# Routed experts taken in the rank order of their counts, with 512 to 336 slots by rank, in a kernel of power attention and a mixture of experts

## What is computed

```python
scores = softmax(x @ gate_w.T)                    # x: N = 4096 rows of D = 256; E = 64 experts
topk_w, topk_idx = top_k(scores, 6)               # 6 experts per row, weights normalized to sum 1
flat_e = topk_idx.reshape(-1)
order = argsort(flat_e); se = flat_e[order]; st = order // 6
counts = bincount(flat_e, length=E)
pos = arange(A) - offsets[se]; valid = pos < 768  # a row past slot 768 of its expert is dropped
buf[se, pos] += x[st]                             # E x 768 x 256
g, u = buf @ w_gate.T, buf @ w_up.T               # F = 176 hidden columns per expert
eo = (silu(g) * u) @ w_down.T
y[st] += eo[se, pos] * weight                     # scattered back, added
return y + shared(x)                              # one shared expert of 352 hidden columns, all rows
```

## Time and profile before

| | us |
|---|---|
| median of 3 runs | 2335.61 |
| lowest, highest | 2334.75, 2338.43 |
| span of the profiled execution | 2331.3 |
| PE busy | 2202.9 (94%) |
| PE weight loads busy | 1988.1 (85%) |
| DVE busy | 1327.8 (57%) |
| ACT busy | 1202.7 (52%) |
| POOL busy | 817.4 (35%) |

### The profile page before, as it was taken

One profiled execution on the slowest core, in us unless ns is written; L12 is line 12 of the kernel. 1 busy time (PEld: TensorE's weight loads), 2 busy tenths in 40 slices (PEclk: granted clock), 3 DMA queues, 4 the chain that ended last, 5 costly groups with the idle time before them and its releaser, 6 DMA issues.

```text
span 2331.3 us, 38666 instructions
## 1 busy us (share of the span) xinstructions
PE 2202.9 (94%) x14776; PEld 1988.1 (85%) x14776; DVE 1327.8 (57%) x2873; ACT 1202.7 (52%) x2232; POOL 817.4 (35%) x792
## 2 busy tenths in 40 slices
PE   8999999999999999999999999998888999999980
PEld 7999998998989899898988889997777888888870
DVE  3444444454655454555545475447657888888863
ACT  4545444454444454444445444444345777777763
POOL 3111112000014500002440014400445888878785
PEclk9999999999999999999999999999999999999995
DMA  5866721122113222111322213211548988898857
GB/s 179 330 256 261 298 80 60 45 61 84 50 54 119 89 57 76 54 51 59 120 85 79 66 54 100 90 61 61 185 149 267 213 203 213 195 214 194 212 70 235
DMA packets 153136, 310.61 MB, mean 133 GB/s; under 512 B 26576, under 2 KB 88272, under 8 KB 152944
## 3 DMA queue, kind: packets, MB, share of 16 engines
q1 hardware_dynamic: 104320, 251.98, 32.3%
q0 software_dynamic: 48192, 55.68, 12.3%
q10 hardware_dynamic: 432, 0.40, 0.0%
HBM read 168.01 MB, written 149.34 MB: 136 GB/s over the span
## 4 chain that ended last, share of the span: by engine, by line
PE 87%; DVE 5%; issue 3%; ACT 2%; POOL 1%; DMA 1%; another core or an unknown queue 0%; ACTq 0%; POOLq 0%; SPq 0%; DVEq 0%
PE bank L856 53%; PE bank L1219 20%; PE bank L866 8%; PE bank L1322 2%; PE bank L1232 2%; DVE ub L1724 1%; POOL y_part L2125 1%; DVE stats L2038 0%; ACT q_hi L1447 0%; POOL slots L2115 0%; ACT x1t_hi L1489 0%; POOL xt_lo L2077 0%; DMA gw_raw<-in_gw 0%; DMA y_part<-y_e,row_token 0%; DVE bank L1908 0%
## 5 line engine op out<-in xcount | busy, mean ns | idle before, releaser
L1219 PEld LDWEIGHTS bank<-v,a 128*128 128x128 f32 x4608 | 603.4, 191 | 43.8 <-ACT a L1471 0.8
L1219 PE MATMUL bank<-v,a 128*128 128x129 f32 x4608 | 616.9, 275 | 0.6 <-ACT a L1471 0.6
L2125 POOL DMA_INDIRECT y_part<-y_e,row_token x264 | 414.1, 1569 | 105.9 <-issue 85.9
L2095 POOL TENSOR_TENSOR decay_all<-decay_all,tab 128x128 f32<-128x128 f32 x128 | 60.9, 476 | 917.2 <-DMA decay_all<-decay_dram 916.8
L1467 ACT ACTIVATE a<-bank,c_s 128x512 f32<-128x512 f32 x384 | 263.0, 685 | 178.3 <-PE bank L856 163.1
L1471 ACT ACTIVATE a<-ub 128x512 f32<-128x512 f32 (+1 forms) x256 | 133.8, 524 | 377.1 <-DVE ub L1724 359.2
L2115 POOL DMA_INDIRECT slots<-rows,slot_u x192 | 188.7, 983 | 308.2 <-PE bank L1219 137.3
L856 PE MATMUL bank<-q_hi,k_hi 128*128 128x512 f32 (+1 forms) x640 | 261.8, 409 | 8.3 <-DVE ub L1724 7.3
L1703 DVE TENSOR_TENSOR q_lo<-bank,q_hi 128x512 fp32r<-128x512 f32 x128 | 88.5, 691 | 273.7 <-ACT q_hi L1447 270.3
L856 PE MATMUL bank<-q_lo,k_hi 128*128 128x512 f32 (+1 forms) x640 | 237.5, 371 | 0.0
L856 PE MATMUL bank<-q_hi,k_lo 128*128 128x512 f32 (+1 forms) x640 | 236.5, 370 | 0.0
(11 more groups left out here) (215 smaller groups left out, 4917.5 us busy)
## 6 DMA issues: line engine op xcount, KB each, us to landing
slots<-acc SPq DMA_DIRECT2D x65, 816.0 KB, 7.9
w_raw_f<-in_wffn SPq DMA_DIRECT2D x66, 624.0 KB
xr<-slots SPq DMA_DIRECT2D x64, 544.0 KB
decay_all<-decay_dram SPq DMA_DIRECT2D x128, 128.0 KB
w_hi<-w_dram SPq DMA_DIRECT2D x24, 384.0 KB
w_lo<-w_dram SPq DMA_DIRECT2D x24, 384.0 KB
sum<-y_part SPq DMA_DIRECT2D x14, 512.0 KB, 10.2
wc_hi<-wc_dram SPq DMA_DIRECT2D x24, 256.0 KB
```

Source lines behind the costliest of these rows:

```text
L1219: ins = e.matmul(dst[:, tt, r, :], a32[u % NA][:, r, t0:t0 + P], v[n % 3][:, s, :], start=(s == 0 and r == 0), stop=(s == 2 * g + tt), ski ...
L2095: e.tensor_tensor(arg[:, GROUP:GROUP + P], arg[:, P:GROUP], mask, ALU.add)
L2125: e.indirect_dma_start(out=y_part[part], out_offset=bass.IndirectOffsetOnAxis(ap=token, axis=0), in_=y_e[y][:, j, :], in_offset=None, boun ...
```

## The change

**Ranks.** When `taken` has the counts of the first seven eighths of the rows, DVE makes a key per expert (`rank_keys`: expert number minus 64 times its count). It takes the diagonal to have each expert's key on its partition, and counts the smaller keys in its row. That is the expert's rank, 0 for the fullest. A one-hot matrix of ranks goes to PE, which multiplies it with the expert numbers (`rank_experts`), and DVE copies the product out. `rank_i` then holds the expert of each rank, on one partition, for address registers, and `rank_x` the same on all partitions.

**Tiles by rank.** `TIERS` gives each rank its tiles: ranks 0 to 17 four of 128 slots, 18 to 37 four of 112, 38 to 51 three of 128, 52 to 63 three of 112. That is 512, 448, 384 and 336 slots. Ranks 0 to 3 get one more step each, of one tile of 128 (slots 512 to 639), with the weights of the step before it. `SEQ` takes wide and narrow ranks in turn: 0, its extra, 63, 1, its extra, 62, and so on, then 4, 59, 5, 58, to 31, 32: 68 steps.

**Transfers.** SP loads the rank's expert number into a register (`value_load`) ahead of each transfer of rows or weights and forms the address from it (`rows_at`, `weights_at`). The extras' rows come by such plain transfers too (`extra_in`), and all four are issued in step 0. `over_in`, its 12 fetches on POOL, `counted`'s scan and `jobs` are gone.

**General path.** In step 2, `rank_counts` multiplies the final counts out by rank on PE, and DVE compares them with the reach of each rank (640, 512, 448, 384, 336). `rest_i` says for each group of four ranks whether one of them is over, `over_count` how many are. If it is not zero, every group with an expert over its reach runs four bodies, each over the slots from its reach to 768, behind the last step. `KEPT`, the number of steps whose slot weights are kept, goes from 8 plus 4 to 12. `slots` and its filling shrink from 65 to 64 regions.

Its core:

```diff
+TIERS = [(18, 4, P), (20, 4, 112), (14, 3, P), (12, 3, 112)]
+MAIN_TILES = [(nt, pt) for n_, nt, pt in TIERS for _ in range(n_)]
+EXTRA = 4
+REACH = [nt * pt + P * (x_ < EXTRA) for x_, (nt, pt) in enumerate(MAIN_TILES)]
-OVER_AT = 18, 34, 50, E + 3
-SEQ = list(range(E))
-for i_, place_ in enumerate(OVER_AT):
-    SEQ.insert(place_, E + i_)
+MAINS = [x_ for i_ in range(E // 2) for x_ in (i_, E - 1 - i_)]
+SEQ = [y_ for x_ in MAINS for y_ in ((x_, E + x_) if x_ < EXTRA else (x_,))]
...
     route_some(3)
+    do("rank_keys")
     do("gate_up", 2, 0)
+    on_spare("rank_experts")
     route_some(2)
...
-    do("jobs", 0)
...
-        after = SEQ[place + 1:place + 4]
-        if 3 <= place < 2 + JOBS // JC:
-            do("jobs", place - 2)
-        if x_id + 2 < E:
-            do("rows_in", x_id + 2)
+        later = MAINS[NTH[x_id] + 2:NTH[x_id] + 4] if x_id < E else []
+        if later:
+            do("rows_in", later[0])
         if place == 0:
-            for i in range(KJ):
-                do("over_in", E + i)
+            for i in range(EXTRA):
+                do("extra_in", E + i)
+        if place == 2:
+            on_spare("rank_counts")
             do("load_count")
...
+            def expert_at(x_id):
+                once.wait_ge(c_rank, 1)
+                return e.value_load(rank_i[0:1, x_id % E:x_id % E + 1], min_val=0, max_val=E - 1)
+
             def rows_in(x_id):
-                e.dma_start(xr[r][:, :, :], slots[x_id * CAP:x_id * CAP + MAIN, :].rearrange(
-                    "(p j) c -> p j c", p=P)).then_inc(c_r[r], 16)
+                e.dma_start(xr[i][0:pt, 0:nt, :], rows_at(expert_at(x_id), 0, nt, pt)).then_inc(c_r[i], 16)
...
+            def down_rows(ps, k, w, tiles, pt):
+                for jj, j in enumerate(tiles):
+                    ins = down_passes(e, [(k % HS, w)], slice(j * pt, (j + 1) * pt), ps[0:pt, jj * C:(jj + 1) * C], jj == 0)
...
+            def rank_keys():
+                once.wait_ge(*out_of(("route", B - 1, "taken")))
+                step(e.scalar_tensor_tensor(out=rank_key, in0=taken[:, :], scalar=-float(E), in1=tab[:, K_IOTA:K_IOTA + E],
+                                            op0=ALU.mult, op1=ALU.add))
+                step(diagonal_sum(rank_key, rank_col[:, 0:1]))
+                steps_done()
+                step(e.tensor_scalar(rank_cmp, rank_key, rank_col[:, 0:1], None, ALU.is_lt))
+                steps_done()
+                step(e.tensor_reduce(rank_col[:, 1:2], rank_cmp, AX.X, ALU.add))
+                steps_done()
+                e.tensor_scalar(rank_hot[:, :], tab[:, K_IOTA:K_IOTA + E], rank_col[:, 1:2], None, ALU.is_equal).then_inc(c_hot)
+
+            def rank_experts():
+                once.wait_ge(s_spare, m + 1)
+                e.tensor_copy(rank_i[:, :], bank[6 + m % 2][0:1, 0:E]).then_inc(c_rank)
+                e.tensor_copy(rank_x[:, :], bank[6 + m % 2][:, 0:E]).then_inc(s_out_of[m % 2])
...
+                pt = shape_of(x_id)[1]
+                for j in tiles_in_pair(x_id, pair):
+                    add_rows(row_token[kept_at(x_id)][0:pt, j:j + 1], y_e[PLACE[x_id] % YS][0:pt, j, :], pt, part, c_add[part])
...
-            with e.If(count > KJ):
+            with e.If(count > 0):
+                for q0 in range(0, E, REST):
+                    with e.If(e.value_load(rest_i[0:1, q0 // REST:q0 // REST + 1], min_val=0, max_val=1) > 0):
+                        for q in range(q0, q0 + REST):
+                            body(q)
```

More of the change, by code:

```diff
@@ L530, in schedule @@
         do("hidden", k, 3)
-        if len(after) > 1:
-            do("split_lo", after[1], 2)
+        if later:
+            do("split_lo", later[0], 2)
         if place:
@@ L536, in schedule, with shape_of, pairs_of, tiles_in_pair @@
     return order, spare
+def shape_of(x_id):
+    return MAIN_TILES[x_id] if x_id < E else (1, P)
 def tiles_of(x_id):
-    return MT if x_id < E else OVER_TILES
+    return shape_of(x_id)[0]
+def pairs_of(x_id):
+    return (tiles_of(x_id) + 1) // 2
+def tiles_in_pair(x_id, pair):
+    return range(2 * pair, min(2 * pair + 2, tiles_of(x_id)))
 def before_job(x_id, count):
@@ L607, in build @@
     N_SPLIT = len(split_at)
-    down_of = {x_id: spare["down", x_id, tiles_of(x_id) // 2 - 1] for x_id in range(E + KJ)}
+    down_of = {x_id: spare["down", x_id, pairs_of(x_id) - 1] for x_id in SEQ}
     shared_down_of = {m: spare["shared_down", m, 1] for m in range(M)}
@@ new lines, in over_body @@
+                for i, tiles in enumerate(pairs):
+                    e.wait_ge(s_spare, m + i + 1)
+                    turned_hi(bank[6 + (m + i) % 2], 0, tiles, pt)
+                e.wait_ge(o_rest[q // REST], rest_moved(q) + 32)
+                e.activation(wf_hi[w][:, :], w_rest_raw[:, :], ACT.Copy).then_inc(c_wh)
+                for part in range(4):
+                    hidden_part(k, part, nt * pt)
+                e.wait_ge(c_pick, STEPS + q + 1)
+                md = m + len(pairs)
@@ L1594, in over_skip_banks, with over_skip @@
-            def over_skip_banks(first, count):
-                for q in range(first, first + count):
-                    for j in range(OVER_TILES):
-                        e.sem_inc(s_out_of[(over_m(q) + 1 + j) % 2], 1)
+            def over_skip(first, last):
+                e.sem_inc(c_xh, (over_m(last) - over_m(first)) // 2)
+                e.sem_inc(c_wh, last - first)
+                e.sem_inc(c_silu, 2 * (last - first))
+                e.sem_inc(c_hh, 2 * (last - first))
+                for i in range(2):
+                    e.sem_inc(s_out_of[i], rest_downs(first, last, i))
@@ L1951, in pick_weights @@
-            def pick_weights(nth_, x_rows, n, expert, out_):
-                once.wait_ge(c_pick, nth_)
-                step(e.scalar_tensor_tensor(out=of_expert[:, 0:n, :], in0=x_rows[:, 0:n, ID_COL:ID_COL + TOPK], scalar=expert,
-                                            in1=x_rows[:, 0:n, W_COL:W_COL + TOPK], op0=ALU.is_equal, op1=ALU.mult))
-                steps_done()
-                e.tensor_reduce(out_[:, 0:n], of_expert[:, 0:n, :], AX.X, ALU.add).then_inc(c_pick)
+                diagonal_sum(taken[:, :], count_col[:, :]).then_inc(c_hot)
@@ new lines, in rank_counts @@
+            def rank_counts():
+                m = spare["rank_counts",]
+                once.wait_ge(s_spare, m + 1)
+                e.tensor_tensor(rank_over[:, :], bank[6 + m % 2][0:1, 0:E], tab[0:1, K_REACH:K_REACH + E], ALU.is_gt).then_inc(
+                    s_out_of[m % 2])
+                once.wait_ge(*out_of(("rank_counts",)))
+                e.tensor_reduce(rest_i[:, :], rank_over[:, :].rearrange("p (g r) -> p g r", r=REST), AX.X, ALU.max)
+                step(e.tensor_reduce(rank_col[0:1, 0:1], rank_over[:, :], AX.X, ALU.add))
+                steps_done()
+                e.tensor_copy(over_count[:, :], rank_col[0:1, 0:1]).then_inc(c_count)
@@ L2010, in over_body @@
+                e.wait_ge(o_step, q + 1)
+                e.tensor_reduce(row_w[KEPT][0:pt, 0:nt], of_expert[0:pt, 0:nt, :], AX.X, ALU.add).then_inc(c_pick)
+                for part in range(4):
+                    hidden_part(k, part, nt * pt)
+                for i in range(len(pairs)):
+                    e.wait_ge(s_out_of[(m + i) % 2], (m + i) // 2 + 1)
+                e.wait_ge(c_wl, N_SPLIT + q + 1)
+                e.wait_ge(c_pick, STEPS + q + 1)
                 e.wait_ge(c_h, 2 * (k + 1))
@@ L2219, in pool_program @@
             all_sent(once)
-        FILLS = [(slots[ex * CAP:(ex + 1) * CAP, :], slot0[:, :, :]) for ex in range(E + 1)]
+        FILLS = [(slots[ex * CAP:(ex + 1) * CAP, :], slot0[:, :, :]) for ex in range(E)]
         N_FILL = len(FILLS)
@@ L2345, in constants @@
     t[:, K_IOTA:K_IOTA + E] = np.arange(E)
-    for i, first in enumerate((MAIN, MAIN + P, 0)):
-        t[:, K_ROW + i] = first + np.arange(P)
+    t[:, K_REACH:K_REACH + E] = [reach if reach < CAP else N for reach in REACH]
+    t[0:E, K_EXPERT] = np.arange(E)
     return t
```

479 lines of the change are left out of this document (233 added, 246 removed).

## The result

The change takes 2281.7 us (median of 4 runs, 2278.4 to 2282.8) where the kernel before takes 2336.2: a ratio of 0.9767, 95% interval 0.9752 to 0.9781. So 54 us went, where I forecast 75. The measured time lies inside the range (2244 to 2286), next to its upper end, and 10 us from the first rival's 2272 against 22 from the forecast.

The account below looks back on a forecast made before the run. PE was taken to bound the kernel, four others within 20%. PE -68.5, POOL's tail -12.9 and the ranks +6 sum to -75.4 us, from 2335.6 to 2260 us; range 2244 to 2286.

Parts of the forecast that it names:

- the first rival: Routed experts: POOL's add costs the same at 112 rows as at 128; 2272 us, chance 0.25.
- PE's part, -68.5: Routed experts: fewer columns and no `jobs` cut PE's work to 431 us, 68.5 us less.
- The prices on the line: PE's products of 448, 384 and 336 columns start 0.204, 0.176 and 0.154 us apart, between the 256- and 512-column prices.
- 0.111 for 128 columns: PE's products in the extra steps: 0.111 us each, from a 129-column product in attention; the line would give 0.063.
- TensorE at 1.2 GHz inside the expert part: Sign listed under what would show the forecast wrong: PE at the lower clock during the routed experts.
- The ranks, +6: Ahead of the routed experts: DVE waits for PE's rank product, so the layer norm's statistics start 6.6 us later; +6 us.
- POOL's tail, -12.9: From PE's last gate-and-up product to the flag behind the last add: shrinks from 33.4 to 20.5 us.
- 2.6 us of leftover lag: End of the routed part: POOL's remaining lag, counted as 2.6 us within the 20.5 us tail.
- The fixed add: POOL in the routed part: an add of 112 rows costs as much as one of 128; 2272 us, chance 0.25.
- DVE's round: Three-tile steps: DVE's round stays at 6.58 us however few the slots; 2290 us, chance 0.1.
- The general path: Behind the last step: one expert over its rank's reach costs four bodies, 88 us; 2348 us, chance 0.03.
- DMA work: DMA engines in the routed part: work falls with rows and adds to about 370 us of 431.

Follow-up runs that it names:

- d1: The kernel before, unchanged, measured and traced again on the chip of the third batch: 0.9986 of the kernel before's time.
- d2: The change, unchanged, measured and traced again on the chip of the third batch: 0.9780 of the kernel before's time.
- a2: The change with its pairs of ranks reversed, from the middle outwards (31, 32 first, 0 and 63 last): 0.9731 of the kernel before's time.
- a4: The change with one add of rows left out for each of the 20 experts with four tiles of 112: 0.9687 of the kernel before's time.
- b1: The change with ranks in their own order, 0 to 63, instead of wide and narrow in turn: 0.9812 of the kernel before's time.
- a1: The change with PE's product for the ranks ahead of gate_up(2, 0) instead of behind it: 0.9761 of the kernel before's time.
- a3: The change with tiles of 128 where it has 112, the same 234 adds: 0.9785 of the kernel before's time.
- d3: The change with four tiles of 128 (512 slots) for every rank, on the third batch's chip: 0.9998 of the kernel before's time.

## Why the prediction was right, and where a step failed

- **PE's part, -68.5: measured -64.5.** The prices on the line held (0.20, 0.18, 0.16 us), and so did 0.111 for 128 columns. A pair of 448-column steps is cheaper than I had it (13.58 for 13.86), one of 512 and 336 dearer (12.85 for 12.66). What was missing are waits in the first steps: 4.21 us for the first extra's rows, for which I had 3, 1.66 for `xe_lo` behind the extra, and 3.4 for evictions, for which I had 1. The sign "TensorE at 1.2 GHz inside the expert part" was seen, from 1769.4 to 1779.6, where the granted clock is 0.50. It is no loss against before, which has 10.3 us of this kind (1759.5 to 1762.9, 1773.1 to 1780.0) with 9.2 us of PE's work in them; in the change it is 6.0.
- **The ranks, +6: measured +5.0** (138.0 against 133.1) in the first pair of traces and 10.5 in the pair d1, d2. The mechanism is as forecast: DVE waits 5.0 us for a product that stands behind six others, and the statistics come 6.8 us later relative to `taken` (6.6 forecast). That 5.0 came so near to 6 is in part luck, as the stretch behind the statistics scatters by more than that (134.0 to 141.5 for one order of work). What scatters are the granted clock and pauses of PE that no releaser ends. In a2, the shortest, the clock from 1660 to 1700 is 1.00 and the pauses sum to 4.2 us; in d2 they are 0.87 and 8.0.
- **POOL's tail, -12.9: measured +0.6. This is the step that failed.** The price of an add was nearly right (1.51 for 112 rows, where I had taken 1.46, 1.57 for 128), and so was the sum of the adds: 234 of them with 0.30 between come to 430.5 us where I had 425. What was wrong is the sentence built on it, that POOL is "level with PE, so it no longer falls four buffers behind". A level total doesn't keep a queue short. The order puts the pairs with eight adds last, where POOL loses 0.9 us on each of six, and before them it has no slack to make good a pause (1.6 and 3.8 us here, and in other traces of this order a lag of 10 to 18 us at rank 17). The sum should have been made pair by pair, along the order, as the lag. In place of the 2.6 us of leftover lag that I took for the tail the runs show about 15: 14 by the lags, and by a4, an estimate from its tail, 15.
- **The fixed add (0.25, 2272)** is nearer to what happened. An add of 112 rows takes 1.51, closer to 1.57 than to 1.37. By the Trainium skill (DMA: Bandwidth & Descriptors, Anatomy of one DMA, the SWDGE path) many descriptors can be emitted before their incremental cost shows; the trace agrees to the extent that 16 rows of 128 change an add by 4%. That the flag came at 2237.5 and not at 2229 is from pauses and a later first add (1787.4).
- **DVE's round (0.1, 2290)** did not happen: in the change no step beyond the first few waits for `xe_lo`, and even in rank order three-tile steps run at 5.6 to 5.8 us (b1).
- **The general path** never ran, and register loads cost SP nothing that shows.
- **DMA work**: I had it fall with rows and adds to 370 us of 431. It fell less: over the routed part the share is 0.85 of 499 us before and 0.91 of 435 in the change, 424 us and 396, and the bytes went from 101.9 to 93.5 MB. Between 1900 and 2100 the share is 97% or 98%. PE waits for nothing there, so DMA didn't bind PE. Whether it makes POOL's pauses at 2016 and 2027, whose releaser the profile doesn't name, is open. The longer one is 3.8, 4.8 and 3.8 us in the change, a1 and a4, and 2.2 in a3; no run took the traffic away.

The range held because its upper end was made to take in the fixed add with 10 us of waits. That is width, and not a right account of POOL: of the 21 us by which the sum was off, 13.5 are the tail, 4 PE's part and 4.4 the scatter ahead of `taken`, less 1 of the ranks.

## What to carry to other kernels

Where two engines are level in total, make the sum along the order and follow the lag of the second: its tail is decided by the steps that come last, and a pause anywhere stays in it unless there is slack behind. Put the work that loads the trailing engine first and the work on which it can catch up last; here turning the order round, with two small edits, took 20 us more, where 57 us saved on PE (from d3 to d2) had made the tail 15 longer. Cutting slots shrinks what is paid per column, not what is paid per instruction or per real row.
